# One exponential for the whole power in a 2048-step recurrence, with the exponent joined last

## What is computed

```python
def step(h, inp):                        # h: [B=2, D=256, N=16, 2], complex numbers
    x_t, dt_t, B_t, C_t, xr_t = inp
    h_carrier = h.mean(axis=1)
    T = jnp.cos((c_phase(xr_t) - c_phase(h_carrier)) / 2.0) ** 2
    alpha = jnp.exp(dt_t[..., None] * A_neg)
    expo = 1.0 + (1.0 - alpha) * 0.5 * (1.0 - T[:, None, :])
    mag, ph = (c_mag(h), c_phase(h))
    cmag = jnp.minimum(jnp.exp(expo * jnp.log(mag + 1e-08)), 10.0)
    h = from_polar(cmag, ph)
    h = h + B_t[:, None, :, :] * (dt_t * x_t)[:, :, None, None]
    h = from_polar(jnp.tanh(c_mag(h)), c_phase(h))
    y_t = jnp.einsum('bnc,bdnc->bd', C_t, h)
    return (h, y_t)
```

## Time and profile before

| | |
|---|---|
| median of three runs | 13085.53 us (13085.5 to 13089.1) |
| profiled execution, its own span | 13078.4 us |
| stretch of the recurrence in it | 267 to 9808 us, 9541 us |
| DVE busy in that stretch | 7493.5 us (79%) |
| ACT busy in that stretch | 6591.7 us (69%) |
| one step in its regular course | 4.64 us |

### The profile page before, as it was taken

How to read it: one execution, slowest core, us unless ns; L and a number is a source line. 1 busy time by engine, 2 the same in 40 slices (tenths; PEclk the granted TensorE clock), 3 DMA queues, 4 the chain that set the end, 5 groups by cost and what they waited for, 6 DMA issues and landing times. The chain is left out here.

```text
span 13078.4 us, 218367 instructions
## 1 busy us (share of the span) xinstructions
PE 5746.3 (44%) x52526; PEld 4265.9 (33%) x52542; DVE 9955.2 (76%) x54539; ACT 8368.0 (64%) x42451; POOL 94.6 (1%) x164
## 2 busy tenths in 40 slices
PE   5222222222222222222222222222227978888998
PEld 5222222222222222222222222222224546753335
DVE  5777777777777777777777777777773957968874
ACT  6666666666666666666666666666663733254666
POOL 0000000000000000000000000000000100000000
PEclk8555555555555555555555555555557988998999
DMA  1000100001000000000010000100000000001100
GB/s 55 14 14 14 21 14 14 14 14 20 14 14 14 14 17 17 14 14 14 14 20 14 14 14 14 20 14 14 14 14 14 1 13 16 1 27 56 30 23 21
DMA packets 339443, 227.40 MB, mean 17 GB/s; under 512 B 27662, under 2 KB 324183, under 8 KB 337884
## 3 DMA queue, kind: packets, MB, share of 16 engines
q1 hardware_dynamic: 338140, 213.30, 7.6%
HBM read 187.41 MB, written 25.43 MB: 16 GB/s over the span
## 5 line engine op out<-in xcount | busy, mean ns | idle before, releaser
L533 PE MATMUL scan_p_car<-scan_hs,scan_mean_mat 32*32 32x2 f32 x16392 | 578.3, 198 | 6837.1 <-DVE scan_hb L660 6824.1
L533 PEld LDWEIGHTS scan_p_car<-scan_hs,scan_mean_mat 32*32 32x32 f32 x16392 | 401.5, 135 | 7016.7 <-DVE scan_hb L660 7003.6
L578 ACT ACTIVATE scan_act_ps<-scan_act_ps 128x64 f32<-128x64 f32 (+1 forms) x8193 | 1642.6, 200 | 64.6
L578 ACT ACTIVATE scan_act_ps<-scan_r 128x64 f32<-128x64 f32 x2048 | 466.2, 228 | 1873.2 <-DVE scan_r L657 1873.2
L560 PE MATMUL scan_p_y<-scan_c_masked,scan_hb 128*64 128x4 f32 x16384 | 1234.5, 253 | 0.0
L538 PE MATMUL scan_p_car<-scan_eps_row,ones 1*128 1x3 f32 x4102 | 1198.0, 360 | 39.3 <-DMA scan_a_log<-L_attn_a_A_log 39.1
L578 ACT ACTIVATE scan_cm<-scan_dl,scan_s 128x64 f32<-128x64 f32 x2049 | 712.0, 347 | 729.6 <-DVE scan_s L683 729.6
L657 DVE TENSOR_TENSOR scan_c<-scan_V,scan_cm 128x64 f32<-128x64 f32 x4096 | 738.1, 221 | 470.1 <-ACT scan_cm L578 425.3
L560 PEld LDWEIGHTS scan_p_y<-scan_c_masked,scan_hb 128*64 128x64 f32 x16384 | 1055.4, 216 | 34.8
L538 PEld LDWEIGHTS scan_p_car<-scan_eps_row,ones 1*128 1x128 f32 x4102 | 1020.2, 307 | 72.1 <-DMA scan_a_log<-L_attn_a_A_log 39.5
L660 DVE SCALAR_TENSOR_TENSOR scan_uw<-scan_w,scan_rsq 128x64 f32<-128x64 f32 x2048 | 459.5, 224 | 660.3 <-ACT scan_rsq L578 654.7
(11 more groups left out here) (450 smaller groups left out, 17413.5 us busy)
## 6 DMA issues: line engine op xcount, KB each, us to landing
scan_step_in<-scan_scratch SPq DMA_DIRECT2D x520, 256.0 KB, 6.0
qk_scratch<-qkv_parts SPq DMA_DIRECT2D x32, 384.0 KB, 2.5
attn_qT<-qk_scratch SPq DMA_DIRECT2D x192, 64.0 KB, 2.2
attn_kT<-qk_scratch SPq DMA_DIRECT2D x192, 64.0 KB, 2.2
scan_scratch<-prep_dts SPq DMA_DIRECT2D x32, 256.0 KB, 2.1
x<-L_attn_a_x SPq DMA_DIRECT2D x1, 4096.0 KB
out<-x SPq DMA_DIRECT2D x1, 4096.0 KB
filter_in_taps<-c_kT SPq DMA_DIRECT2D x1, 2048.0 KB
```

Source lines behind the costliest of these rows:

```text
L533: last = nc.tensor.matmul(p_car[slot][rows, 0:2], mean_mat[rows, :], hs[rows, :], start=False, stop=True)
L578: nc.scalar.activation(dst, src, func, **kw).then_inc(counts[par]["act"], 1)
```

## The change

The change rewrites the power. Before, the exponential gave only the factor `mag ** (expo - 1)` and `mag` was multiplied in by `F`; its exponent came from `dl` and the per-partition `s`, which was the exponential's scale operand. Now one exponential gives `C = mag ** expo` from a finished exponent `y`:

- two DVE operations per step, `am = alpha - 1` and `be = 1.25 - 0.25 * alpha`, are issued right behind the `bx` products (function `powers`);
- `dl`, `F` and `s` are gone. In their place DVE makes `y2 = lm * be`, `dd = lm * dot * am` and `y = dd * rs + y2`. `dot` and `rs` are one number per partition, read through a pointer as the scalar of a scalar_tensor_tensor;
- `V = hb * ru`, which no longer needs `mag`, and `c = V * C`. `C` takes `y` with no scale operand;
- `mag` lies in PSUM instead of SBUF;
- ACT's order was `mag, lnh, nsq, lm, lnn, ru, rs, cm` and is `mag, nsq, lm, lnn, lnh, rs, ru, C`.

The core of the diff:

```diff
@@ -404,8 +404,8 @@
-DVE_STEP = ["c0", "c1", "w0", "w1", "sq0", "sq1", "r2", "n2", "bx0", "bx1", "uw0", "uw1", "h0", "h1", "nh", "hp", "dot", "dl", "F", "s", "V"]
-ACT_STEP = ["al", "l", "M", "ln2", "E", "rsq", "L1", "R", "th2", "l2", "mag", "lnh", "nsq", "lm", "lnn", "ru", "rs", "cm"]
+DVE_STEP = ["c0", "c1", "w0", "w1", "sq0", "sq1", "r2", "n2", "bx0", "bx1", "am", "be", "uw0", "uw1", "h0", "h1", "nh", "hp", "dot", "y2", "dd", "y", "V"]
+ACT_STEP = ["al", "l", "M", "ln2", "E", "rsq", "L1", "R", "th2", "l2", "mag", "nsq", "lm", "lnn", "lnh", "rs", "ru", "C"]
...
@@ -583,20 +585,20 @@
                     op(par, l2[:, :], th2[:, :], ACT.Ln, bias=EPS_MAG)
                     after(act, "act", "l2", par, k)
                     op(par, mag[:, :], l2[:, :], ACT.Exp, scale=0.5)
-                    after(act, "dve", "nh", par, k)
-                    op(par, lnh[:, :], nh[:, :], ACT.Ln)
                     after(act, "pe", "carrier", par, k)
                     op(par, squares[:, :], p_car[slot][:, 0:3], ACT.Square, accum_out=nsq[:, :])
                     after(act, "act", "mag", par, k)
                     op(par, lm[:, :], mag[:, :], ACT.Ln, bias=EPS_MAG)
                     after(act, "act", "nsq", par, k)
                     op(par, lnn[:, :], nsq[:, :], ACT.Ln)
+                    after(act, "dve", "nh", par, k)
+                    op(par, lnh[:, :], nh[:, :], ACT.Ln)
+                    after(act, "act", "lnn", par, k)
+                    op(par, rs[:, :], lnn[:, :], ACT.Exp, scale=-0.5)
                     after(act, "act", "lnh", par, k)
                     op(par, ru[:, :], lnh[:, :], ACT.Exp, scale=-0.5)
-                    after(act, "act", "lnn", par, k)
-                    op(par, rs[:, :], lnn[:, :], ACT.Exp, scale=-0.5)
-                    after(act, "dve", "s", par, k)
-                    op(par, cm[:, :], dl[:, :], ACT.Exp, scale=s_[:, 0:1])
+                    after(act, "dve", "y", par, k)
+                    op(par, C[:, :], y[:, :], ACT.Exp)
@@ -675,14 +677,19 @@
                     after(dve, "act", "nsq", par, k)
                     stt(sem, products[:, :], p_car[slot][:, 0:2], 1.0, tab[:, nxt, k_nxt, 2:4], ALU.mult, ALU.mult, accum_out=dot[:, :])
                     after(dve, "act", "lm", par, k)
-                    stt(sem, dl[:, :], alpha[:, (k + 1) % 2, :], 1.0, lm[:, :], ALU.subtract, ALU.mult)
+                    tt(sem, y2[:, :], lm[:, :], be[:, :], ALU.mult)
+                    after(dve, "dve", "dot", par, k)
+                    stt(sem, dd[:, :], lm[:, :], dot[:, 0:1], am[:, :], ALU.mult, ALU.mult)
+                    after(dve, "act", "rs", par, k)
+                    after(dve, "dve", "dd", par, k)
+                    stt(sem, y[:, :], dd[:, :], rs[:, 0:1], y2[:, :], ALU.mult, ALU.add)
                     after(dve, "act", "ru", par, k)
-                    stt(sem, F[:, :], mag[:, :], EPS_MAG, ru[:, :], ALU.add, ALU.mult)
-                    after(dve, "act", "rs", par, k)
-                    after(dve, "dve", "dot", par, k)
-                    nc.vector.tensor_scalar(s_[:, :], rs[:, :], dot[:, 0:1], -0.25, ALU.mult, ALU.add).then_inc(sem, 1)
-                    after(dve, "dve", "F", par, k)
-                    tt(sem, V[:, :, :], hb[:, slot, 0:2, :], F[:, :].unsqueeze(1).to_broadcast([P, 2, J]), ALU.mult)
+                    tt(sem, V[:, :, :], hb[:, slot, 0:2, :], ru[:, :].unsqueeze(1).to_broadcast([P, 2, J]), ALU.mult)
+
+                def powers(sem, k):
+
+                    nc.vector.tensor_scalar(am[:, :], alpha[:, (k + 1) % 2, :], 1.0, None, ALU.subtract).then_inc(sem, 1)
+                    nc.vector.tensor_scalar(be[:, :], alpha[:, (k + 1) % 2, :], -0.25, 1.25, ALU.mult, ALU.add).then_inc(sem, 1)
@@ -716,10 +725,10 @@
                         for k in range(CS):
                             slot = k % 2
                             nxt, k_nxt = following(par, k)
-                            after(dve, "act", "cm", par, k - 1)
+                            after(dve, "act", "C", par, k - 1)
                             after(dve, "dve", "V", par, k - 1)
                             for comp in range(2):
-                                tt(sem, c[:, comp, :], V[:, comp, :], cm[:, :], ALU.mult)
+                                tt(sem, c[:, comp, :], V[:, comp, :], C[:, :], ALU.mult)
                             for comp in range(2):
                                 after(dve, "dve", f"c{comp}", par, k)
                                 tt(sem, w[:, comp, :], c[:, comp, :], bx[:, comp, :], ALU.add)
@@ -735,6 +744,8 @@
                                 dve.wait_ge(tab_in, n + 2)
                                 dve.sem_inc(taken, 1)
                             b_products(sem, nxt, k_nxt)
+                            after(dve, "act", "al", par, k)
+                            powers(sem, k)
                             if k and k % YS == 0:
                                 output(par, n * CS, k - 1)
                             after(dve, "act", "rsq", par, k)
```

More of the change, by code:

```diff
@@ L449, in scan_phase @@
         c, w, sq, uw, bx, V = (ph.sb(n, [P, 2, J]) for n in ("c", "w", "sq", "uw", "bx", "V"))
-        r2, n2, rsq, R, th2, nh, lm, dl, mag, ru, F, cm = (
-            ph.sb(n, [P, J]) for n in ("r2", "n2", "rsq", "R", "th2", "nh", "lm", "dl", "mag", "ru", "F", "cm"))
+        r2, n2, rsq, R, th2, nh, lm, ru, C = (
+            ph.sb(n, [P, J]) for n in ("r2", "n2", "rsq", "R", "th2", "nh", "lm", "ru", "C"))
+        am, be, dd, y2, y = (ph.sb(n, [P, J]) for n in ("am", "be", "dd", "y2", "y"))
         act_ps = [ph.ps(f"act_ps{k}", [P, 512]) for k in range(2)]
-        lr, E2, ln2 = (act_ps[0][:, q * J:(q + 1) * J] for q in range(3))
+        lr, E2, ln2, mag = (act_ps[0][:, q * J:(q + 1) * J] for q in range(4))
         M, L1, l2, lnh = (act_ps[1][:, q * J:(q + 1) * J] for q in range(4))
@@ L456, in scan_phase @@
         squares, nsq, lnn = act_ps[1][:, 256:259], act_ps[1][:, 260:261], act_ps[0][:, 260:261]
-        dot, s_, rs = (ph.sb(n, [P, 1]) for n in ("dot", "s", "rs"))
+        dot, rs = (ph.sb(n, [P, 1]) for n in ("dot", "rs"))
         p_car = [ph.ps(f"p_car{k}", [P, 512]) for k in range(2)]
@@ L462, in scan_phase @@
         tab_in, mask_in, bx_first, al_first = ph.sem("tab_in"), ph.sem("mask_in"), ph.sem("bx_first"), ph.sem("al_first")
+        powers_first = ph.sem("powers_first")
         y_out, left, cleared, taken = ph.sem("y_out"), ph.sem("left"), ph.sem("cleared"), ph.sem("taken")
@@ L708, in _ @@
                 dve.wait_ge(al_first, 1)
+                powers(powers_first, CS - 1)
+                dve.wait_ge(powers_first, 2)
                 after_state(1, CS - 1, 1)
```

## The result

The changed kernel takes 13367.6 us (median of 4 runs, 13362.8 to 13372.1) against 13085.6 us before (4 runs, 13085.5 to 13089.1). The ratio is 1.0214, with a 95% interval of 1.0199 to 1.0228: slower by 282 us. The forecast was slower by 82 us, 13167, with a range of 13050 to 13240. The sign was right; the size was not, and the time lies outside the range.

The account below looks back on a forecast made before the run. The prediction took a dependent chain across engines in the 2048 recurrence steps as the bound, no engine being full. +0.07 for the longer way and -0.03 for the squares gave +0.04 us a step, +82 us: 13167, range 13050 to 13240.

Parts of the forecast that it names:

- +0.07 for the way from there to `c`: From the start of the squares to the next `c`: 1.44 us instead of 1.37 in each step.
- `products` to `dd`: DVE, counted from the squares' start: `products` starts at 0.24 us, `y2` at 0.38, `dd` at 0.52.
- `dd` and `y` at 0.28 each: DVE, in series on the chain: each takes 0.28 us, of which 0.055 is for reading a pointer.
- the two rivals with free pointers: Pointers in `dd` and `y` both hidden: 12942 us, chance 0.09; only `dd`'s hidden: 13055 us, chance 0.08.
- `y` starts at 0.835: DVE: `dd` ends 0.80 us behind the squares' start and `y` starts a release of 0.035 later.
- The squares, -0.03: ACT, with `lnh` no longer ahead: squares start 0.03 us earlier a step, the middle of 0 and 0.06.
- gains nothing: Lower bound for the squares on ACT: they waited for PE all along, so the new order gains 0 us.
- `C` at 0.256: ACT's exponential without a scale pointer takes 0.256 us, as `th2` does, where `cm` took 0.35.
- `V` 0.08 under `C`: `V`, behind `y` on DVE, would let `c` go at 1.36 us, 0.08 under `C`.
- `am` and `be` hidden at `uw`: The two new DVE operations fit the 0.34 us idle time ahead of `uw` and cost nothing.
- the two rivals fall that made DVE's own work count: DVE's own work sets the time: 14066 us, chance 0.02; the cover at `uw` fails: 13515 us, chance 0.03.
- Loop code, at most 3 us: DVE's program grows by two instructions a step; its 38.1 us of issue waits grow 8%, 3 us at most.

Follow-up runs that it names:

- the first experiment: The changed kernel with the two waits of `y` exchanged, `dd` first and `rs` second; 13203.3 us, ratio 1.0089 to the kernel before.
- The fourth experiment: The changed kernel with `y`'s waits exchanged, plus constants in place of the pointers `dot` and `rs` in `dd` and `y`; 12966.5 us, ratio 0.991.
- the second: The kernel before with the two waits of `c` exchanged, `V` first and `cm` second; 13226.4 us, ratio 1.0108.
- the fifth experiment: The changed kernel with `y`'s waits exchanged, plus `am` and `be` computed once and not in each step; 13201.6 us, ratio 1.0087 to the kernel before.
- the last two experiments: New version with two exponentials, most work ahead of the carrier, 12755.8 us; the same without storing `hb`'s first component, 12681.8 us; ratios 0.9747 and 0.9698 to the kernel before.

## Why the prediction was right in sign and wrong in size

The forecast of a step was -0.03 for the squares and +0.07 for the way from there to `c`, +0.04 in sum. Measured are 0.134. The sign was not luck: with the wait that was overlooked put right, the first experiment is still 116 us slower than before, and inside the range. Point by point:

- **`products` to `dd`**, the spacings behind the accumulator's read and between independent instructions: right to 0.01.
- **`dd` and `y` at 0.28 each**: right, 0.279 and 0.285 in the groups of after. The fourth experiment shows that both pointers are paid in full, so the two rivals with free pointers fall.
- **`y` starts at 0.835**: this step failed. The rule behind it was "a dependent one by the length of the first and a release", with 0.03 to 0.04 for a release "wherever it is seen". Its own rows have 0.06 from DVE to PE (7.02 to 7.08), so "wherever" was too much. The rows that the rule was taken from, `s` to `cm` and `cm` to `c`, are instructions whose last wait is their only one or the one written first. `y`'s last wait is the one written second, and it cost 0.115. The first experiment puts 164 us on it, of the 200 by which the forecast was short; the second shows the same effect, 139 us, in the kernel before. I had the code with the two waits in front of me; in the order of instructions that I read, waits don't stand, and I added up durations only.
- **The squares, -0.03**: they came 0.025 earlier, but took 0.16 instead of 0.14, so `products` was only 0.011 earlier. That is 0.019 a step less gain than forecast, 39 us, and it accounts for the 36 us by which the first experiment lies over the forecast (13203 to 13167). The bound "gains nothing" rested on the earlier trace rows, read as PE's late release, and there is another reading. The trace has in ACT's queue, at that line, a small instruction of its own ahead of each of the 16 (columns as at L473):

```profile
L336 ACTq FUSED_REGOPS  x16: 46/48/57, 59.3 to 207.4; - x16
```

  The wait there is made in a loop against a counter in a register. In the step of the earlier trace rows the small instruction starts 0.035 behind the shown end of PE's product, and ACT's starts 0.10 behind that. By this most of the 0.13 is the price of that form of wait and not of PE, a gap of the same sort as the one in `y`. It is argued from the trace, in which PE's end is modelled; no run tests it.
- **`C` at 0.256**: right. The estimate by the Trainium skill ("ScalarE: Activation LUTs", section "What ACT_TABLE_LOAD costs"), 0.239, was too low.
- **`V` 0.08 under `C`**: `V` was over at 6.58 and `C` at 6.67 in the step above, 0.09 apart. Right.
- **`am` and `be` hidden at `uw`**: right, shown by the fifth experiment to within 2 us. With it the two rivals fall that made DVE's own work count.
- **Loop code, at most 3 us**: the wait for issue did not grow (38.1 before, 37.9 after). But some 10 us are in longer steps at fixed places of the loop, for which the forecast had no term. Their cause was not found. Taking `am` and `be` out moved the places but left their number (120 of 0.1 to 0.4 us over the median in the first experiment and in the fifth).

The range failed because of the same step: its upper end held only the bounds of the squares, rounded up. Starts behind a producer's end had been seen at 0.03, 0.06 and 0.13, and only the first was used for `y`.

## What to carry to other kernels

Where an instruction waits for two things, write first the wait that ends last; in these kernels the other became a small instruction of its own, which is free only if its producer is over early. By the 0.115 and 0.036 on DVE, an estimate is 0.08 us ahead of the other; at 0.02 ahead, on ACT, it still showed. In a chain of dependent small instructions add up releases and pointers as well as lengths: at 128x64 a scalar read through a pointer cost 0.06 us on DVE and 0.09 on ACT each time it was on the path, so apply it once, late, and compute ahead all that does not need it. Busy time added in an engine's gap cost nothing here, with DVE at 84%, so look at which wait ends last and not at the share.

## What the hardware showed that was not expected

- A separate wait that ends last costs 0.07 to 0.08 us over one that stays with the instruction: 0.115 against 0.035 on DVE for a producer on DVE, 0.10 against 0.03 for one on ACT. Its own record is only 21 ns long.
- A small ACTIVATE (128x3 from PE's result) took 0.14 where it followed `lnh` by 0.15, and 0.16 where it started 0.35 behind PE's start, as early as in any run. So half of an earlier start was lost again. In the last two experiments it stands behind `lnh` too, but starts 0.35 behind PE's start, and takes 0.16; so it is not the neighbour that makes the difference.
- A pointer's price on DVE is in the length and in the spacing: 279 to 220 ns and 285 to 225, and `y` started 0.26 behind `dd` instead of 0.32 (the fourth experiment against the first).
- The steps longer than the median recur at the same places of the written-out loop in each of its 8 turns, 16 places after the change and 8 before; the cause is not shown.
